# Reordering the start of a fused conv, int8 product and mixture kernel: agg_weights and conv(1) ahead of a weight transpose, one input load later

## The reference

```
x = x + ffn0(cond0(x, cond_128))    # layer 0
x = x + ffn1(cond1(x, cond_128))    # layer 1
```

## Time and profile before

| what | value |
|---|---|
| median of 3 runs | 648.43 us (648.33 to 648.83) |
| the profiled execution's own time | 648.43 us |
| its span | 646.6 us |
| TensorE (PE) busy | 623.8 us, 96% |
| VectorE (DVE) busy | 418.3 us, 65% |
| ScalarE (ACT) busy | 335.3 us, 52% |
| GpSimd (POOL) busy | 336.2 us, 52% |
| mean granted TensorE clock | 0.989 |

### The profile page before, as it was taken

One profiled execution on the slowest core, in us unless ns is written; L12 is line 12 of the kernel. 1 busy time (PEld: TensorE's weight loads), 2 busy tenths in 40 slices (PEclk: granted clock), 3 DMA queues, 4 the chain that ended last, 5 costly groups with the idle time before them and its releaser, 6 DMA issues.

```text
span 646.6 us, 14948 instructions
## 1 busy us (share of the span) xinstructions
PE 623.8 (96%) x5865; PEld 337.3 (52%) x5898; DVE 418.3 (65%) x891; ACT 335.3 (52%) x566; POOL 336.2 (52%) x223
## 2 busy tenths in 40 slices
PE   7789999999999999999999999999999999999997
PEld 5556565566566666656554444444444444444443
DVE  5958778877787778787537797745544433444434
ACT  2857898667778777776652436334333313333100
POOL 3012222217778522225485689886866678666400
PEclk8799999999999999999999999999999999999999
DMA  8969877677799797764529014554555433457103
GB/s 299 361 137 365 295 284 273 233 266 276 280 342 336 285 359 280 259 229 140 217 73 357 35 34 153 206 203 156 196 195 193 158 132 136 162 197 259 66 1 130
DMA packets 46707, 138.38 MB, mean 214 GB/s; under 512 B 13180, under 2 KB 13468, under 8 KB 46465
## 3 DMA queue, kind: packets, MB, share of 16 engines
q1 hardware_dynamic: 41886, 120.65, 52.6%
q10 hardware_dynamic: 4752, 16.78, 6.4%
HBM read 89.13 MB, written 48.28 MB: 213 GB/s over the span
## 4 chain that ended last, share of the span: by engine, by line
PE 51%; DVE 1%; issue 0%; ACT 0%; DVEq 0%
PE ps L770 36%; PE ps L584 9%; PE ps L752 2%; PE ps L521 2%; PE ps L505 1%; PE ps L462 0%; PE ps L552 0%; DVE z_lo L1304 0%; DVE unscale L1441 0%; DVE ring L1293 0%; DVE yb L1245 0%; DVE zT L1306 0%; PE ps L555 0%; PE ps L730 0%; PE ps L493 0%
## 5 line engine op out<-in xcount | busy, mean ns | idle before, releaser
L1088 POOL TENSOR_TENSOR x<-x_in,f_both 128x512 f32<-128x512 f32 x64 | 74.0, 1157 | 195.9 <-DVE f_both L1277 195.9
L521 PE MATMUL ps<-wqT,yq_both 128*128 128x512 bf16 x479 | 113.2, 379 | 6.0 <-issue 4.6
L462 PE MATMUL ps<-x_ph,conv_w 64*64 64x256 f32 (+1 forms) x1024 | 98.2, 396 | 2.2 <-DMA conv_w<-in_conv_taps 2.0
L863 ACT ACTIVATE yv<-yb,yinv 128x128 f32<-128x128 f32 x256 | 78.0, 389 | 2.3 <-DVE yinv L1268 2.2
L902 ACT ACTIVATE ring<-ring,ratio 128x2048 f16<-128x2048 f16 x26 | 50.6, 1994 | 51.1 <-DVE wst L1537 14.1
L770 PE MATMUL ps<-ffn_wT,ring 128*128 128x512 f16 x312 | 71.6, 379 | 0.0
L462 PEld LDWEIGHTS ps<-x_ph,conv_w 64*64 64x64 f32 (+1 forms) x1024 | 51.1, 137 | 37.4 <-issue 14.2
L521 PEld LDWEIGHTS ps<-wqT,yq_both 128*128 128x128 bf16 x512 | 45.2, 97 | 48.4 <-issue 1.0
L1245 DVE TENSOR_TENSOR yb<-ps,ybias 128x1024 f32<-128x1024 f32 x32 | 39.1, 1223 | 41.1 <-PE ps L462 41.0
L584 PE MATMUL ps<-ffn_wT,ring 128*128 128x512 f16 x288 | 64.6, 379 | 0.0
L856 ACT ACTIVATE ring<-ps,t_up 128x512 f16<-128x512 f32 x64 | 40.5, 683 | 45.5 <-issue 38.1
(11 more groups left out here) (284 smaller groups left out, 1096.6 us busy)
## 6 DMA issues: line engine op xcount, KB each, us to landing
x_ph<-in_x_phases SPq DMA_DIRECT2D x32, 516.0 KB, 6.1
x_in<-in_x SPq DMA_DIRECT2D x32, 512.0 KB, 6.4
x_scratch<-x SPq DMA_DIRECT2D x32, 512.0 KB, 2.8
x_scratch<-ring SPq DMA_DIRECT2D x26, 512.0 KB, 4.1
ring<-x_scratch SPq DMA_DIRECT2D x26, 512.0 KB, 4.3
wst<-in_w_rows SPq DMA_DIRECT2D x12, 512.0 KB, 5.0
x_in<-x_scratch SPq DMA_DIRECT2D x12, 512.0 KB, 6.5
out<-x_in ACTq DMA_DIRECT2D x12, 512.0 KB, 3.6
```

The costliest lines, as they stand in the source:

```text
L462: return mm(ps_conv[o, g * 2 * MB:(g + 1) * 2 * MB], conv_w[k, g, w.start + o.start:w.start + o.stop], xp[k, g, :, view], start=first, sto ...
L521: last = mm(acc_bank(t, h), yqT[:, t % 2, p, :], wqT[:, p, h * HALF:(h + 1) * HALF], start=p == 0, stop=p == PH - 1)
L863: last = A(yv[:, s, :], yb[:, t % 2, s, :], ACT.Copy, scale=yinv[:, s:s + 1], bias=MAGIC)
L1088: g.tensor_tensor(x1[:, t % 2, s], x_in[:, t % 3, s], f16[:, s], ALU.add).then_inc(sem("x1_ready"), 1)
```

## The change

The change gives four of the engines' lists another order in the stage ahead of the loop; every operation stays, with two numbers changed on semaphores and four more small matmuls in a warm. On SyncE's queue the second tile's convolution input, load_phases(1), goes behind wq block 4, and the four small kw loads go ahead of wq block 3. On TensorE conv(1) and agg_weights go ahead of wq_transposed(2); the waits that keep the shared banks apart follow the new order (agg_weights waits for two copied blocks instead of three, and wq_transposed(2) instead of (3) waits for two agg_out). On ScalarE the first two agg_out go ahead of scale_rows(0) and wq_out(2). On VectorE chan_max and scales of tiles 0 and 1 go later, behind one or more steps of the weight blocks.

```diff
@@ SyncE
             load_wq(2)
-            load_phases(1)
-            load_wq(3)
             for g in range(4):
                 sp.dma_start(kw[g]...)
+            load_wq(3)
             sp.dma_start(pk[:, PACK_1:PACK_W], pack[:, PACK_1:PACK_W]).then_inc(sem("pack2_loaded"), 16)
             load_wq(4)
+            load_phases(1)
             load_wq(5)
@@ TensorE, in wq_transposed and agg_weights
-                if o == 3:
+                if o == 2:
                     pe.wait_ge(sem("agg_ready"), 2)
...
-                pe.wait_ge(sem("wqT_ready"), 3)
+                pe.wait_ge(sem("wqT_ready"), 2)
@@ TensorE
             wq_transposed(1)
-            warm(12)
+            warm(16)
             max_rows(0)
+            conv(1)
+            max_back(0)
+            agg_weights()
             wq_transposed(2)
-            max_back(0)
-            conv(1)
-            agg_weights()
             pe.wait_ge(sem("pack2_loaded"), 16)
             ... (mixb product, limes transpose)
+            wq_transposed(3)
+            wq_transposed(4)
             max_rows(1)
-            wq_transposed(3)
             tokens_out(0)
-            wq_transposed(4)
+            wq_scales_out(0)
             max_back(1)
             wq_transposed(5)
-            wq_scales_out(0)
+            wq_transposed(6)
             int_product(0, 0)
-            wq_transposed(6)
             wq_transposed(7)
             wq_scales_out(1)
@@ ScalarE
             wq_out(1)
-            wq_out(2)
-            scale_rows(0)
             agg_out(0)
             agg_out(1)
+            scale_rows(0)
+            wq_out(2)
             agg_out(2)
             agg_out(3)
...
             wq_out(3)
+            wq_out(4)
             tokens_sb(0)
-            wq_out(4)
+            wsc_out(0)
             wq_out(5)
-            wsc_out(0)
+            wq_out(6)
             scale_rows(1)
-            wq_out(6)
             wq_out(7)
             wsc_out(1)
@@ VectorE
             wq_round(2)
-            chan_max(0)
             wq_maxima(3)
             wq_scales(3)
+            chan_max(0)
+            wq_inverse(3)
+            wq_maxima(4)
+            wq_round(3)
+            wq_scales(4)
             scales(0)
-            wq_inverse(3)
-            wq_round(3)
-            wq_maxima(4)
-            wq_scales(4)
+            wq_inverse(4)
+            wq_maxima(5)
+            wq_round(4)
+            wq_scales(5)
             conv_bias(1)
-            wq_inverse(4)
+            wq_inverse(5)
             row_max(1)
-            wq_round(4)
-            wq_maxima(5)
-            wq_scales(5)
-            chan_max(1)
-            wq_inverse(5)
             wq_round(5)
-            scales(1)
             wq_maxima(6)
             wq_scales(6)
             wq_inverse(6)
+            chan_max(1)
             wq_round(6)
             wq_maxima(7)
             wq_scales(7)
+            scales(1)
             wq_inverse(7)
             small_maxima()
             wq_round(7)
```

## The result

The changed kernel takes 651.59 us (median of 15 runs, 649.44 to 656.43) against 648.19 for the kernel before (15 runs). The ratio is 1.0053 with a 95% interval of 1.0030 to 1.0076: 1.9 to 4.9 us slower, 3.4 in the middle. 648.9 was forecast, with a range up to 650.6. Two executions of the experiments further down, one of 922 us and one of 1637 us, lie far from all the others and are left out of the ratios there.

What follows compares the result with a forecast made beforehand. TensorE, busy 96% of the span, was taken as the bound, losing time only in a three-engine relay ahead of conv(3). 0 (warm) + 0 (conv(1)'s start) + 0.5 (relay) on 648.43 gave 648.9 us, range 647.3 to 650.6.

Steps and rivals of the forecast that it cites:

- The step that failed: SyncE's mixing-matrix stores, then loads back, load_phases(4) and first w load, start 3.5 us later; costed at nothing.
- The 1 us that I kept for this: Upper-bound allowance for the loop's first loads coming up to 3.5 us later and partly reaching its first iteration.
- Conv(1)'s input: load_phases(1) behind weight block 4 lands at about 18.8, between 18.3 and 19.3; conv(1)'s start costs 0.
- ScalarE's part: Ahead of the loop, agg_out(0) waits for agg_weights; last agg_out at 30.3 against 26.7, tokens_out(0) 3.5 us later, at 30.4.
- the term of the sum for the prologue: Ahead of the loop, up to wq_transposed(7): +0.5 us, moving conv(3) from 44.84 to 45.3.
- rival A: TensorE's clock returns a stretch later or falls again, before conv(1) or at 32.4; about 1.5 us, 650.4 us; chance 0.24.
- rival C: The half-clock stretch at 46 to 49 goes away, conv(3) gains 1.5 us: 647.4 us; chance 0.07.
- The carry into the loop: From conv(3), the loop's start at 44.84 us, a shift goes into the end nearly one to one.

Runs made afterwards that it cites:

- the early load: load_w(0), the loop's first weight-row load, issued ahead of SyncE's wait for the last agg_out; on the changed kernel 648.82 us, on the kernel before 648.26 us.
- the late relay alone: Kernel before, SyncE's mixing-matrix stores, which precede their loads back and load_w(0), also waiting for the sixth copied weight block: 654.18 us, ratio 1.0093.
- filling the wait: Changed kernel with 28 more warm matmuls between max_rows(0) and conv(1), while TensorE waits for conv(1)'s input: 651.06 us, ratio 1.0047.

## Why the prediction was wrong

**The step that failed** is the one on SyncE: "The earlier loads keep the DMA engines busy until past 31 anyway (...), so I cost this at nothing". Two things were wrong in it. The cover by earlier loads is a floor and no reserve. Stores issued at 22.73 or at 26.73 are both done at 33.9 (in one profile, issued at 25.34, at 35.1). For the first that is 11.2 us, with the DMA engines still at 408 GB/s from 30 to 32, which fits a wait behind the older loads. But in the eight profiles with stores issued at 28.5 or later, they take 6.6 to 7.7 us all the same (31.69 to 38.32, 30.79 to 37.70), so the 7.2 us of the kernel before held next to no slack. Of the 5.0 us by which they were late, 4.4 came through. And what is queued behind the relay is not only the mixing data, but an unrelated load on which ScalarE waits in order. I had named load_w(0) as queued behind it and did not follow ScalarE's list past it. The trace of before had the row: ScalarE already waited 1.49 us at w_abs(0). The 1 us that I kept for this had no term in the sum. The step is worth 2.7 of 3.4 us by the early load in the changed kernel, and the late relay alone costs at least as much on the kernel before (2.8 us in its profile, 6.0 by its timed runs).

**Conv(1)'s input** was right: issued at 8.6, landed 10.2 later, at 18.8, conv(1) at 18.86 with the DMA as releaser. The load order alone cost nothing measurable.

**ScalarE's part** was right in its mechanism: it waits for agg_weights (8.55 us; about 5 expected), and tokens_out(0) is released by the last agg_out. It came at 31.8 instead of 30.4, for the most part through the 1.6 us of the half-clock conv(1). In the profile with the early load, where conv(1) ran at full clock, it came at 30.33. int_product(0, 0) and wq_transposed(7), forecast at 34.2 and 36.0, were 0.6 late there (34.84 and 36.63), with no wait for VectorE's wq_round(7) in front, and conv(3) moved by 1.1 instead of 0.5: the term of the sum for the prologue was too small by half a microsecond, as far as that one execution shows.

**The clock, rival A**, happened in the profiled execution, in both places that it named: under conv(1), and at wq_scales_out(0), where full rate came back at about 36. wq_transposed(7) moved by 2.6 instead of 0.5. But it didn't decide the end. conv(3)'s half-rate stretch went away in the same execution (rival C), and filling the wait changed the time by less than the measurement can tell (0.4 us by the ratios, give or take 2). What prologue and clock cost together once the relay is out of the way is better bounded: a ratio of 1.0012 (0.9996 to 1.0028), 0.8 us, between -0.3 and 1.8. That agrees with the 0.5 of the sum and doesn't prove it. So rival A's sign was right for a reason that was not the one that counts, and none of the rivals was the relay.

**The carry into the loop** was wrong in its rule. "Nearly one to one" holds from conv(5) on (583.3 us to the end before and after); between conv(3) and conv(5) a second path, not shifted with TensorE's, joins.

## What to carry to other kernels

When a step moves later, follow every queue that waits for it to the end of what is queued behind it, and then the lists of those who wait for that, also where the data have nothing to do with the step. An idle time of an in-order engine (here 1.49 us at w_abs(0)) can mark a second path with hardly any slack, even when taking it away gains nothing. An independent load is better placed ahead of a wait: here it cost nothing measurable on the kernel before and saved 2.7 us on the changed one.

## What the runs showed of the hardware

The same first instructions ran at a different clock from one execution to the next. conv(0), with an unchanged TensorE list ahead of it, took between 2.98 and 4.98 us in the twelve profiles, and conv(3) took 4.50 in the kernel before and 2.98 in the same kernel with only the load order changed. Whether the end follows depends on what comes next. In the changed kernel conv(0) took 2.98, but conv(1) then waited for its input. In the kernel before with the early load it took 2.98 too, conv(1) started at 17.44 instead of 18.85 and conv(5) at 61.44 instead of 63.34, and that execution, 646.61 us, was the fastest of its kernel. The Trainium skill, TensorE: Matmul & The Clock Gate, What's actually happening, says that the clock's activity window runs free and is not reset at a kernel's start. The trace agrees as far as that the point of change moves between executions. A single profile of a short prologue is therefore one draw, and I had read the half-rate stretches of one as a property of the kernel.
